# Reciprocals of the attention denominators, spread over channels by a trip through DRAM instead of by matmul

## The reference, cut to what matters

```python
q = jax.nn.elu(q) + 1.0
k = jax.nn.elu(k) + 1.0
kv = k * v
k_cumsum = jnp.cumsum(k, axis=1)
kv_cumsum = jnp.cumsum(kv, axis=1)
denom = jnp.einsum('bthd,bthd->bth', q, k_cumsum)
denom = jnp.clip(denom, EPS, None)[..., None]
y = q * kv_cumsum / denom
y = y.reshape(Bsz, Tlen, C)
return jnp.einsum('btc,ec->bte', y, Wproj) + bproj
```

## Time and profile before

| | |
|---|---|
| median of 3 runs | 2354.07 us (2353.47 to 2354.6) |
| profiled execution, span from first to last instruction | 2352.2 us |
| profiled execution, own time around the span | none is given beside the span |
| PE busy | 2332.6 us, 99% of the span |
| DVE, ACT, POOL busy | 1652.7 us (70%), 1144.1 us (49%), 451.6 us (19%) |
| DMA | 354.77 MB, 151 GB/s over the span |
| matmuls of the spread (line 1103) | 64, 4 for each batch |

### The profile page before, as it was taken

How to read it: one execution, slowest core, us unless ns; L and a number is a source line. 1 busy time by engine, 2 the same in 40 slices (tenths; PEclk the granted TensorE clock), 3 DMA queues, 4 the chain that set the end, 5 groups by cost and what they waited for, 6 DMA issues and landing times.

```text
span 2352.2 us, 34307 instructions
## 1 busy us (share of the span) xinstructions
PE 2332.6 (99%) x12060; PEld 1927.6 (82%) x12060; DVE 1652.7 (70%) x2863; ACT 1144.1 (49%) x1902; POOL 451.6 (19%) x395
## 2 busy tenths in 40 slices
PE   9999999999999999999999999999999999999998
PEld 7878888888888888888888888888888888888787
DVE  8886685866858668586675867758677586875643
ACT  5354445454454544545455444545454454554543
POOL 1112211121121212212122111211113111121200
PEclk9999999999999999999999999999999999999999
DMA  9255445463444634446354454544536435453332
GB/s 341 83 160 188 117 144 163 133 218 106 150 155 143 207 102 179 132 144 206 108 182 133 138 193 126 187 127 143 180 117 206 117 135 179 126 161 99 100 116 90
DMA packets 97276, 354.77 MB, mean 151 GB/s; under 512 B 11858, under 2 KB 11986, under 8 KB 86994
## 3 DMA queue, kind: packets, MB, share of 16 engines
q1 hardware_dynamic: 80210, 319.02, 38.2%
q0 software_dynamic: 16896, 33.56, 9.0%
HBM read 329.47 MB, written 23.07 MB: 150 GB/s over the span
## 4 chain that ended last, share of the span: by engine, by line
PE 92%; DVE 1%; ACT 1%; issue 1%; POOL 0%; DMA 0%; SPq 0%; POOLq 0%; DVEq 0%; ACTq 0%
PE acc L1274 29%; PE m L1049 13%; PE h_ps L1250 10%; PE h_ps L1252 10%; PE h_ps L1251 10%; PE m L1079 6%; PE m L1133 2%; PE m L1210 2%; PE m L1117 2%; PE m L1118 2%; PE m L1119 2%; PE m L1231 1%; PE m L1090 1%; PE m L1103 1%; PE acc L1290 0%
## 5 line engine op out<-in xcount | busy, mean ns | idle before, releaser
L561 ACT ACTIVATE hid<-h_ps,b 128x512 f32<-128x512 f32 x252 | 173.6, 689 | 598.2 <-PE h_ps L1252 597.5
L1049 PE MATMUL m<-xT_hi,wq 128*128 128x512 f32 x1320 | 408.2, 390 | 0.3 <-DVE xT_lo L1010 0.3
L1250 PE MATMUL h_ps<-x2T_hi,we_hi 128*128 128x512 f32 x1008 | 400.4, 397 | 2.4 <-DVE x2T_lo L905 2.4
L1274 PE MATMUL acc<-we_hi,h_hi 128*128 128x512 f32 x1008 | 400.8, 398 | 1.5 <-DVE h_lo L921 1.5
L921 DVE TENSOR_TENSOR h_lo<-hid,h_hi 128x512 fp32r<-128x512 f32 x252 | 224.3, 890 | 252.9 <-ACT h_hi L568 252.9
L1252 PE MATMUL h_ps<-x2T_hi,we_lo 128*128 128x512 f32 x1008 | 392.9, 390 | 0.0
L1274 PE MATMUL acc<-we_hi,h_lo 128*128 128x512 f32 x1008 | 392.8, 390 | 0.0
L1274 PE MATMUL acc<-we_lo,h_hi 128*128 128x512 f32 x1008 | 392.7, 390 | 0.0
L1251 PE MATMUL h_ps<-x2T_lo,we_hi 128*128 128x512 f32 x1008 | 392.4, 389 | 0.0
L911 DVE TENSOR_TENSOR we_lo<-raw,we_hi 128x1024 fp32r<-128x1024 f32 x256 | 319.9, 1250 | 31.2 <-ACT we_hi L551 31.2
L499 ACT ACTIVATE e_f<-m,sb_qkv,scale 128x512 f32<-128x512 f32 x116 | 90.5, 780 | 479.8 <-PE m L1079 477.7
(11 more groups left out here) (259 smaller groups left out, 3368.6 us busy)
## 6 DMA issues: line engine op xcount, KB each, us to landing
raw<-in_w SPq DMA_DIRECT2D x256, 512.0 KB, 4.2
wq<-wq_scratch SPq DMA_DIRECT2D x168, 512.0 KB, 3.3
x<-in_x_tok SPq DMA_DIRECT2D x16, 1024.0 KB, 5.5
x<-in_b_proj POOLq DMA_DIRECT2D x16, 1024.0 KB, 14.7
ctx_T<-in_ctxT SPq DMA_DIRECT2D x16, 1024.0 KB, 8.2
x<-in_b POOLq DMA_DIRECT2D x16, 1024.0 KB, 11.8
ctx_tok<-in_ctx_tok SPq DMA_DIRECT2D x15, 1024.0 KB, 4.7
out_dram<-x SPq DMA_DIRECT2D x15, 1024.0 KB, 4.8
```

Source lines behind the costliest of these rows:

```text
L561: act.activation(hid[:, f % 2, :], up_bank(b, f)[:, :], ACT.Relu, bias=b1[:, b % 2, f:f + 1]).then_inc(h_done, 1)
L1049: pe.matmul(bank(a, j)[:, :], w[:, s, t, :], x_hi[:, t, :], start=(t == 0 and s == 0), stop=False)
L1250: pe.matmul(ps, we_hi[:, g % NW, js], x2T_hi[:, j, :], start=(j == 0), stop=False)
L1274: last = pe.matmul(acc[t][:, :], hx[:, f % 2, ts], wx[:, g % NW, C:], start=(f == 0 and n == 0), stop=(f == FC - 1 and n == 2))
```

## The change

For batches 2 to 14 (13 of the 16) the spread by matmul goes. ACT stores the reciprocals to a DRAM scratch in step 20 (four DMAs, 16 rows of 512 B each), and at the end of step 21, once the stores have landed, issues four loads of 256 KB that bring each head's row of 512 numbers to the 32 partitions of its channels, into `xT_lo`, which is free then. For this the channels are laid out so that partition p of a tile belongs to head p modulo 4: weights and biases are permuted on the host, and `head_sum` is built from the identity by one DVE sum and four POOL copies at the start. DVE multiplies the first two tiles at the end of step 22 and the last two in step 23. In batches 3 to 14 the high parts, low parts, projection, `CTX_SUM`, `SPLIT_X` and `NORM_1` come one step later than before, or two (`LOW`); batch 2 had those slots already. Batches 0, 1 and 15 keep the matmul and their slots.

```diff
+SPREAD_BY_DMA = range(2, NB - 1)
...
+def turn(b):
+    return min(b, SPREAD_BY_DMA.start)
+
+
+def reciprocals_before(b):
+    return 2 * turn(b) + b
...
-SPREAD = plan(21, 20, 21, 22)
-HIGH = plan(22, 20, 21, 23)
-LOW = plan(23, 21, 23, 25)
-PROJECT = plan(25, 23, 25, 26)
-CTX_SUM = plan(26, 25, 26, 27)
-SPLIT_X = plan(29, 28, -6, 30)
-NORM_1 = plan(31, 29, 30, 32)
+SPREAD = plan(22, 20, 21)
+SPREAD[NB - 1] = 21
+HIGH = plan(23, 20, 21)
+HIGH[NB - 1] = 22
+LOW = plan(25, 21, 23)
+LOW[NB - 1] = 23
+PROJECT = plan(26, 23, 25)
+PROJECT[NB - 1] = 25
+CTX_SUM = plan(27, 25, 26)
+CTX_SUM[NB - 1] = 26
+SPLIT_X = plan(30, 28, -6)
+SPLIT_X[NB - 1] = 29
+NORM_1 = plan(32, 29, 30)
+NORM_1[NB - 1] = 31
...
+        def spread_rows(a, cc):
+            return rden_dram[a, XH * cc:XH * cc + XH, :].unsqueeze(0).broadcast_to([HD, XH, T])
...
-        MADE = 11
+        MADE = 13
...
+            pool.wait_ge(fourth_done, 1)
+            for cc in range(CC):
+                pool.tensor_copy(head_sum[:, cc, :].rearrange("p (r h) -> p r h", r=2)[:, :, XH * cc:XH * cc + XH],
+                                 fourth[:, :].unsqueeze(1).broadcast_to([P, 2, XH])).then_inc(made, 1)
...
+                if (a := at(i, h, RALL)) is not None and a in SPREAD_BY_DMA:
+                    act.wait_ge(rden_done, reciprocals_before(a) + 1)
+                    for s in range(TT):
+                        act.dma_start(rden_dram[a, :, s * P:s * P + P], rden[s * SEG:s * SEG + NH, :]).then_inc(rden_st, 16)
...
+                    if (a := at(i, h, RALL + 1)) is not None and a in SPREAD_BY_DMA:
+                        act.wait_ge(rden_st, 16 * TT * (a - SPREAD_BY_DMA.start + 1))
+                        for n in range(2):
+                            for cc in range(2 * n, 2 * n + 2):
+                                act.dma_start(y_lo(a)[:, cc, :].bitcast(F32),
+                                              spread_rows(a, cc)).then_inc(rden_in[n], 16)
...
+                if a in SPREAD_BY_DMA:
+                    return
...
             def times_reciprocal(a, cc):
-                dve.wait_ge(rb_mm, CC * a + cc + 1)
+                if a not in SPREAD_BY_DMA:
+                    dve.wait_ge(rb_mm, CC * turn(a) + cc + 1)
+                else:
+                    dve.wait_ge(rden_in[cc // 2], 32 * (a - SPREAD_BY_DMA.start + 1))
                 dve.wait_ge(num_done, CC * a + cc + 1)
-                dve.tensor_tensor(numer(a)[:, cc, :], numer(a)[:, cc, :], AB[(cc + 1) % 2][:, :], ALU.mult).then_inc(y_done, 1)
+                rb = AB[(cc + 1) % 2][:, :] if a not in SPREAD_BY_DMA else y_lo(a)[:, cc, :].bitcast(F32)
+                dve.tensor_tensor(numer(a)[:, cc, :], numer(a)[:, cc, :], rb, ALU.mult).then_inc(y_done, 1)
...
                 for n in range(2):
-                    if (a := at(i, h, SPREAD + n)) is not None:
+                    if (a := at(i, h, SPREAD + n)) is not None and (n == 1 or a not in SPREAD_BY_DMA):
                         times_reciprocal(a, 2 * n)
                         times_reciprocal(a, 2 * n + 1)
...
+            dve.wait_ge(made, 7)
+            dve.reduce_sum(fourth[:, :], ident[:, :].rearrange("p (d l) -> p l d", l=XH), AX.X).then_inc(fourth_done, 1)
...
+                    if (a := at(i, h, SPREAD)) is not None and a in SPREAD_BY_DMA:
+                        times_reciprocal(a, 0)
+                        times_reciprocal(a, 1)
...
                 for n in range(2):
-                    if (a := at(i, h, SPREAD + n)) is not None:
+                    if (a := at(i, h, SPREAD + n)) is not None and a not in SPREAD_BY_DMA:
                         spread_reciprocal(a, 2 * n)
                         spread_reciprocal(a, 2 * n + 1)
...
+    order = np.arange(C).reshape(CC, XH, HD).transpose(0, 2, 1).reshape(-1)
+    wq, wk, wv = (w[order] for w in np.split(g["L0_attn_Wqkv"], 3, axis=0))
```

More of the change, by code:

```diff
@@ L101, in build @@
     wq_dram = nc.dram_tensor("wq_scratch", [JOBS, P, 2 * CC * P], F32, kind="Internal").ap()
+    rden_dram = nc.dram_tensor("rden_scratch", [NB, NH, T], F32, kind="Internal").ap()
     with ExitStack() as ctx:
@@ L137, in build @@
         ident, ones, ones_r = sb("ident", [P, P]), sb("ones", [P, P]), sb("ones_r", [P, P], F32R)
-        head_sum = sb("head_sum", [P, CC, SEG])
+        head_sum, fourth = sb("head_sum", [P, CC, SEG]), sb("fourth", [P, XH])
         den, rden = sb("den", [P, P], F32R), sb("rden", [P, P])
@@ L169, in build @@
         mean_ps, route_ps = M2[:, 0:P], M2[0:1, 0:NE]
+        fourth_done = sem("fourth_done")
         made, masks_done, preset, heads_mm = sem("made"), sem("masks_done"), sem("preset"), sem("heads_mm")
@@ L184, in build @@
         kvc_done, q_done, qk_done, num_done = sem("kvc_done"), sem("q_done"), sem("qk_done"), sem("num_done")
+        rden_st, rden_in = sem("rden_st"), [sem("rden_in0"), sem("rden_in1")]
         den_mm, den_max, rden_done, rall_done, rb_mm = (sem(n) for n in ("den_mm", "den_max", "rden_done", "rall_done", "rb_mm"))
@@ L372, in _ @@
                 pool.memset(m[:, :], value).then_inc(made, 1)
-            pool.memset(head_sum[:, :, :], 1.0).then_inc(made, 1)
+            pool.memset(head_sum[:, :, :], 0.0).then_inc(made, 1)
             pool.memset(zeros, 0.0).then_inc(made, 1)
-            twice = head_sum[:, :, :].rearrange("p t (r h) -> p t r h", r=2)
             masks = [(ident[:, :], ALU.not_equal, 1.0, 0, [[-1, P]], 1),
-                     (twice, ALU.is_ge, 0.0, 0, [[P, CC], [0, 2], [-HD, NH]], 1),
-                     (twice, ALU.is_ge, 0.0, HD - 1, [[-P, CC], [0, 2], [HD, NH]], -1),
                      (low_set[:, :], ALU.is_ge, 0.0, -NH, [[-SEG, TT]], 1),
@@ L619, in mix @@
                     normalise(1, c)
[L620 to L624, removed]
+                if (a := at(i, h, RALL)) is not None and a in SPREAD_BY_DMA:
+                    act.wait_ge(rden_done, reciprocals_before(a) + 1)
+                    for s in range(TT):
+                        act.dma_start(rden_dram[a, :, s * P:s * P + P], rden[s * SEG:s * SEG + NH, :]).then_inc(rden_st, 16)
+                if (a := at(i, h, RALL)) is not None and a not in SPREAD_BY_DMA:
+                    act.wait_ge(rden_done, reciprocals_before(a) + 3)
+                    if turn(a) > 0:
+                        act.wait_ge(rb_mm, CC * turn(a))
                     for s in range(TT):
@@ L733, in denominator @@
                 dve.wait_ge(den_mm, a + 1)
-                if (due := upto(a - 1, TT, TT)) is not None:
-                    dve.wait_ge(rall_done, due)
+                if 0 < a <= SPREAD_BY_DMA.start:
+                    dve.wait_ge(rall_done, TT * a)
+                elif a > SPREAD_BY_DMA.start:
+                    dve.wait_ge(rden_st, 16 * TT * (a - SPREAD_BY_DMA.start))
                 dve.tensor_scalar(den[:, :].bitcast(F32), den_ps, EPS_DEN, None, ALU.max).then_inc(den_max, 1)
@@ L739, in denominator @@
                 dve.reciprocal(rden[:, :], den[:, :].bitcast(F32)).then_inc(rden_done, 1)
-                dve.wait_ge(rden_done, 3 * a + 1)
+                if a in SPREAD_BY_DMA:
+                    return
+                dve.wait_ge(rden_done, reciprocals_before(a) + 1)
                 dve.tensor_copy(den[:, :], rden[:, :]).then_inc(rden_done, 1)
-                dve.wait_ge(rden_done, 3 * a + 2)
+                dve.wait_ge(rden_done, reciprocals_before(a) + 2)
                 dve.scalar_tensor_tensor(rden[:, :], den[:, :].bitcast(F32), low_rows[:, 0:1], rden[:, :],
@@ L1095, in spread_reciprocal @@
                 if cc == 0:
-                    pe.wait_ge(rall_done, TT * a + TT)
+                    pe.wait_ge(rall_done, TT * turn(a) + TT)
                     pe.wait_ge(eq_done, 2 * CC * a + 2 * CC)
@@ L1107, in project @@
                     pe.wait_ge(wplo_done, 1)
-                if t < 2:
+                if t < 2 and a not in SPREAD_BY_DMA:
                     pe.wait_ge(y_done, CC * a + 3 + t)
-                else:
+                elif t >= 2:
                     pe.wait_ge(res1_done, TT * a + t - 1)
@@ L1392 @@
                            for w in (wk, wv, wq)], axis=1).reshape(JOBS, P, CC * P),
-        "w_proj": weights(g["L0_attn_Wproj"]).reshape(P, CC * C),
-        "b_qkv": column(g["L0_attn_bqkv"]),
+        "w_proj": weights(g["L0_attn_Wproj"][:, order]).reshape(P, CC * C),
+        "b_qkv": column(g["L0_attn_bqkv"].reshape(3, C)[:, order]),
         "scale": g["L0_attn_scale"].reshape(1, 1),
```

1 line of the change is left out of this document (removed).

## The result

The changed kernel takes **2375.91 us** (median of 6 runs, 2371.07 to 2387.08) against 2354.09 us (2353.31 to 2354.6) of the kernel before: ratio 1.0099, 95% interval [1.0084, 1.0113]. The profiled execution took 2373.42 us, its span is 2371.8, at a granted clock of 0.998. The forecast was 2343.4 with a range of 2341.0 to 2354.0; what happened is rival 2.

The account below looks back on a forecast made before the run. PE, busy 99% of the span, was taken to bound the kernel. Removed matmuls -12.0, `x_sum` +1.3 and everything else 0 gave -10.7 us from 2354.07, so 2343.4 us; likeliest case 2341.0 to 2346, 8-in-10 range ending at 2354.

Parts of the forecast that it names:

- rival 2: The new loads land late enough to make the kernel slower, 2360 to 2378 us; chance 0.12.
- When they land: Step estimating when ACT's stores and loads land: loads between 667.3 and 670.1, taken at 668 with no wait.
- the term of the stores: ACT's 8 KB stores to DRAM land 3.4 us after issue, at 660.6 or 662.3.
- the early case: ACT issues the four stores at once after the reciprocal, by 657.2, and they land at 660.6.
- the late figure: Last load lands at 670.1, behind both `raw` loads, missing the need of 668.7 by 1.4 us.
- When the loads must have landed: Last load must land by 668.7 for `h_lo` to be ready for `down` of step 25; later is paid one for one.
- Removed from PE: Spread matmuls gone from PE: 0.92 us for a batch, 12.0 us over 13 batches (ends 11.8 and 13.0).
- The slots: Later slots, such as `NORM_1` before `GRAM` and the projection before `SPLIT_X`, cost 0.
- Term (a): PE's `MEAN` asks for `x_sum` with almost no margin: 0.1 us for a batch, 1.3 in all (0 to 3.9).
- Term (d): ACT waits for the stores at the end of step 21 with `hidden` of step 22 behind: 0.
- the clock holds unless PE starts to idle: Clock is at the full 2.4 GHz level throughout, so nothing is gained or lost there unless PE idles.

Follow-up runs that it names:

- e6: Changed kernel with denominators, stores and loads one step earlier, `b_proj`'s load issued behind `rstd_of(1, c)` on POOL, and `NORM_2` 50 in place of 51: 2426.06 us.
- e4: Changed kernel with denominators, reciprocal, stores and loads one half step earlier, multiplications left where they are: 2366.53 us.
- e10: Changed kernel with the loads of `x_tok` and `b_proj` issued two steps earlier from batch 3 on: 2358.99 us.
- e7: Changed kernel with all four multiplications behind `h_lo` at the end of step 23 and ACT's high parts one step later: 2354.39 us.
- e12: Changed kernel with `x_tok` and `b_proj` two steps earlier and the four multiplications behind `h_lo`: 2343.04 us.
- e5: Changed kernel without stores and loads (numerators times a constant tile), with `b_proj`'s load issued behind `rstd_of(1, c)` on POOL: 2342.66 us.
- e3: Kernel before with nothing but the changed table of slots, matmul spread kept in all batches: 2353.78 us.
- e2: Changed kernel without stores and loads; DVE multiplies by a constant tile in place of the loaded one: 2348.45 us.
- e9: Changed kernel with the multiplications behind `h_lo` and `b_proj`'s load issued behind `rstd_of(1, c)` on POOL: 2350.85 us.
- e1: Changed kernel whose loads read the rows of the batch before, so they don't wait for this batch's stores: 2366.51 us.
- e8: Changed kernel without stores and loads (constant tile), with one-column matmuls added on PE in steps 21 and 22: 2352.54 us.

## Why the prediction was wrong

**The step that failed is "When they land", and in it the term of the stores.** It put a store at 3.4 us, after the row of `b`. That is a load, issued at 672.5, where the DMA engines are as busy (0.95) but with plain loads alone. In the changed kernel the stores took 5.4 to 6.5 us in batch 5 and 5.9 in the median. So the last one landed 7.9 us after the reciprocal in batch 5, and 8.2 on average, where the two ends of the prediction were 4.8 and 6.5; it was issued as early as the early case had it. The four loads wait for that, and went out from 7.9 to 9.8 in place of from 5.2 or 6.6. From the first issue of a load to the last landing it then took 7.1 us on average (6.1 to 8.9; 8.4 in batch 5), about what the prediction's two ends have for it (6.3 and 7.7). Within this, ACT's four issues took 2.90 us in batch 5, where an issue was taken at SP's 0.34. The prediction put the last landing at 668, which is 12.2 after the reciprocal; it was 16.3 in batch 5 and 15.4 on average.

**What slowed the stores** is in the earlier trace rows, with its 16.0 us: `b_proj`'s accumulating load, which lies across them. The prediction named the `raw` loads only. Without it beside them the stores take 2.5 us (e6), with it 5.0 in the same slots (e4); loads issued close behind it take 11.2 in place of 5.5. The share of the DMA engines does fall where the earlier trace rows have it, to 0.52 at 669 to 671 us (8.8 to 10.8 after the reciprocal); but the late loads were no longer ahead of the second `raw`, as the prediction had it. In batch 5 that was issued at +8.1, ahead of three of the four.

The Trainium skill (DMA: Bandwidth & Descriptors, Issuing engines are not separate DMA queues), by which transfers of several engines share the same DMA engines, was given as speaking for the late figure, 670.1 or 14.3 after the reciprocal. The trace agrees: the last landings are at 14.2 to 16.3, at the late figure or beyond it. The same page's fit for transfers issued from GpSimd (Anatomy of one DMA) would put an 8 KB store at 2.0 us, an estimate from the page; ours, issued from ACT, took 2.5 where `b_proj`'s load was away and 4.7 to 5.9 (medians) where it was not.

**"When the loads must have landed" held.** The need was put at 12.9 after the reciprocal; e10's rounds put it at 13.2. It belongs to the order of DVE's queue, though, not to the data: with the multiplications behind `h_lo` (e7, e12) the need is about 15. The prediction worked out that the projection bears a landing at 669.4 (13.6) and stopped there. It did not ask what `h_lo`, which needs nothing from the loads, was doing behind them.

**"Removed from PE" held**: 12.0 us were forecast, and e5, where nothing else is lost, is 11.5 below before. **The slots** cost 0, as said (e3).

**Term (a), `x_sum`**, was put at 1.3 us (0 to 3.9); it cost 3.0 us in the profiled run (4.5 less the 1.5 that stand at the start) and about 6 in e2. Its mechanism was not the margin of 0.03 us, with which e5's rounds show no wait, but POOL's queue behind `x_tok`.

**Term (d)**, ACT waiting for the stores, was put at 0: ACT stood for 5.19 us ahead of `hid`, which began 10.9 us after the reciprocal (9.5 in e12). That is 1.4 us late, and `h_hi` behind it was still done at 672.41, before DVE came to `h_lo` at 677.68: not on PE's path.

**The balance**, on spans: e5, the same change with nothing lost, is 2340.8, the changed kernel 2371.8. Of the 31.0 us, 22.8 are waits for `h_lo` (25.2 against 2.4 in e5), 3.0 for `x_sum`, and about 3.3 the restart behind a wait (a `down` behind one takes 2.97 us in the chain where it took 2.72, 13 times). Another 1.6 us are the clock: behind the wait of batch 3, eight matmuls of one `down` followed each other every 0.43 us, at the 1.2 GHz level:

```profile
384.00:386.00 2.00, 2.00 (x6) 1.52 (x6) 2.00 (x4) 1.97 (x4) 0.00 (x0) 0.50 0.03 8
```

The prediction had said that the clock holds unless PE starts to idle, and had no term for it. 0.3 us are not placed.

**The chances.** Rival 2 got 0.12, "the loads land late enough to make it slower", 2360 to 2378 us. Its number and its wait are what happened; its sum had the loads slow (9.0 us for 1 MB) and the stores quick, and it was the other way round. The prediction's own late figure already gave a small wait; it chose the early side because the share of the DMA engines falls as the loads begin. The share did fall then, but the stores had used up the margin before the first load went out. A landing with a margin of 0.7 us, out of a sum of five durations of which none was in the trace for this transfer, did not bear 0.52.

What stays open: why one fetch of 16 KB goes with 1.5 us more for 1 MB of `x_tok`; and how the accumulating load slows the others. Taking it off the DMA engines altogether was not tried, nor issuing the loads from another engine than ACT.

## What to carry to other kernels

A trip through DRAM costs two landings in a row and each at the price of the crowd that it meets, not of the stretch where a row for it happens to be: sum both at rows with the same company, and look for a long accumulating load that lies across them. Work that waits for a late transfer belongs in its engine's queue behind everything that doesn't need it; here that order was worth 21.5 us of the median, and issuing `x_tok` and `b_proj` earlier on top of it another 11.4, of which POOL's order alone gives 3.5 (e9), while the three changes of timing without it (e1, e4, e10) all left the kernel slower than before. When a matmul group is taken out or moved, the next delivery that PE asks for is asked for earlier by as much, so its whole chain, up to the loads that hold a queue, is part of the change.

## What the hardware showed beyond expectation

- An issue of a DMA by ACT takes 0.53 to 0.67 us for a load of 256 KB (1.00 once), 0.31 to 0.57 for an 8 KB store, against SP's 0.34; and the four stores go out between ACT's activations that are under way (660.19 lies inside `x`'s).
- Eight matmuls of one column cost 0.81 us of PE's round (e8), 0.10 us each; those of 512 columns cost 0.23. A matmul of one column, which still has a 128 x 128 weight load beside it, is not near free.
- PE idle for 3.13 us (batch 5) kept a granted clock of 1.00; idle for 4.96 us, in e6, it restarted with a mean of 0.62 over the next 4 us, and e6's mean clock is 0.985. The length of the wait alone doesn't settle it: after 1.89 us in batch 3 the clock stood at 0.50, and so it did after 1.97 us in batch 8 of e7.
- The runs of the changed kernel spread over 16 us where those of before spread over 1.3. A part is the clock: the slowest (2387.08 us) has a mean of 0.994 and the fastest (2371.07) 0.998, which is some 9 us, an estimate from the two means. That the rest is how late the crowded transfers land was not measured.
